# Attends and pieces put between the score groups, a new table of pieces, a ring of 28 row tiles

## The reference: what is computed

```python
def _L0_tok_ref(waveform, W, b, ln_gamma, ln_beta):      # 1500 rows of 256 an item
    x = waveform.reshape(B, T // RF, RF)
    h = jnp.einsum('bfr,hr->bfh', x, W) + b
    ...                                                  # layer norm with gamma, beta
    return h * 0.5 * (1.0 + jax.lax.erf(h / jnp.sqrt(jnp.float32(2.0))))
def _L0_attn_ref(x, Wq, bq, Wk, bk, Wv, bv, Wo, bo):     # 16 heads of 16
    Q, K, V = (proj(Wq, bq), proj(Wk, bk), proj(Wv, bv))
    scores = jnp.einsum('bhqd,bhkd->bhqk', Q, K) * scale
    attn = jax.nn.softmax(scores, axis=-1)
    out = jnp.einsum('bhqk,bhkd->bhqd', attn, V)
    ...
    return out @ Wo.T + bo
h = _L0_tok_ref(...)
h = h + _L0_attn_ref(_layernorm(h, axis=-1), ...)
h = h + _L0_ffn_ref(_layernorm(h, axis=-1), ...)         # ends in (y - mu) * rsqrt(var + 1e-05) * ln_g + ln_b
```

## Time and profile before

| what | us |
|---|---|
| time before, median of 3 runs | 2660.03 (2657.61 to 2660.93) |
| the profiled execution, its own time | 2662.67 |
| its span in the profile | 2660.6 |
| PE matmuls busy | 2317.9 (87%) |
| ACT busy | 2124.1 (80%) |
| DVE busy | 1083.9 (41%) |
| POOL busy | 363.6 (14%) |
| mean granted clock of PE | 0.947 of full |

### The profile page before, as it was taken

How to read it: one execution, slowest core, us unless ns; L and a number is a source line. 1 busy time by engine, 2 the same in 40 slices (tenths; PEclk the granted TensorE clock), 3 DMA queues, 4 the chain that set the end, 5 groups by cost and what they waited for, 6 DMA issues and landing times.

```text
span 2660.6 us, 39157 instructions
## 1 busy us (share of the span) xinstructions
PE 2317.9 (87%) x15468; PEld 738.9 (28%) x15468; DVE 1083.9 (41%) x1873; ACT 2124.1 (80%) x1562; POOL 363.6 (14%) x495
## 2 busy tenths in 40 slices
PE   4588998899978998889988899889998899988883
PEld 2222332222222222322223233222222222322221
DVE  6333434534344434443435343453434443442114
ACT  0198887888968888788877888788887888889992
POOL 2201101211021111201112011111102111110002
PEclk7799998999989999899999999899999899999997
DMA  2312211222121222122211221112212022121100
GB/s 63 100 32 70 68 42 40 58 64 65 41 66 31 67 71 57 49 57 63 60 40 49 72 72 43 41 49 72 65 43 63 26 65 74 51 56 43 36 12 29
DMA packets 102228, 144.12 MB, mean 54 GB/s; under 512 B 18439, under 2 KB 81990, under 8 KB 102014
## 3 DMA queue, kind: packets, MB, share of 16 engines
q1 hardware_dynamic: 99478, 139.42, 20.7%
q10 hardware_dynamic: 2536, 1.83, 0.3%
HBM read 55.16 MB, written 61.44 MB: 44 GB/s over the span
## 4 chain that ended last, share of the span: by engine, by line
issue 47%; PE 28%; POOL 10%; ACT 6%; DVE 3%; POOLq 1%; DMA 1%; SPq 1%; DVEq 1%; ACTq 0%
PE PS L744 12%; PE PS L720 8%; PE PS L683 6%; ACT prob L417 5%; POOL sq L329 3%; POOL Y L337 3%; POOL rs L339 2%; POOL rs L310 1%; DMA qk_halves_scratch<-HL 1%; DVE HL L483 1%; PE PS L691 1%; POOLq L338 1%; DVEq L527 1%; DVE HL L485 1%; SPq L209 1%
## 5 line engine op out<-in xcount | busy, mean ns | idle before, releaser
L417 ACT ACTIVATE prob<-PS 125x2000 f32<-125x2000 f32 x768 | 1411.1, 1837 | 136.7 <-PE PS L720 136.6
L744 PE MATMUL PS<-prob,Vst 125*32 125x500 f32 x9216 | 1154.1, 603 | 1.0
L422 ACT ACTIVATE prob<-PS 125x1000 f32<-125x1000 f32 x768 | 772.1, 1005 | 311.1 <-PE PS L720 296.9
L720 PE MATMUL PS<-QA,KA 64*125 64x500 f16 x4608 | 758.6, 409 | 194.6 <-ACT prob L417 140.4
L720 PEld LDWEIGHTS PS<-QA,KA 64*125 64x125 f16 x4608 | 257.0, 134 | 832.0 <-issue 419.9
L744 PEld LDWEIGHTS PS<-prob,Vst 125*32 125x32 f32 x9216 | 220.9, 109 | 536.0 <-issue 356.5
L526 DVE RECIPROCAL On<-Den 128x500 f32<-128x500 f32 x96 | 314.1, 3272 | 67.4 <-DMA Den<-Osb 67.4
L483 DVE TENSOR_SCALAR HL<-PS,b_qk 128x500 f16<-128x500 f32 x96 | 70.9, 739 | 425.8 <-PE PS L683 322.9
L329 POOL TENSOR_TENSOR sq<-HL 128x2000 bf16<-128x2000 f16 x24 | 84.5, 3521 | 981.3 <-DVE HL L485 981.3
L683 PE MATMUL PS<-zT,w_qk 128*128 128x500 f32 x384 | 210.6, 640 | 1.2 <-DVE zT L474 1.2
L710 PE MATMUL PS<-w_o,oT 128*125 128x256 f32 x384 | 122.0, 448 | 57.4 <-DVE Hs L444 35.2
(11 more groups left out here) (72 smaller groups left out, 899.6 us busy)
## 6 DMA issues: line engine op xcount, KB each, us to landing
qk_halves_scratch<-HL SPq DMA_DIRECT2D x384, 125.0 KB
QA<-qk_halves_scratch SPq DMA_DIRECT2D x64, 375.0 KB, 5.2
KA<-qk_halves_scratch SPq DMA_DIRECT2D x64, 375.0 KB, 7.2
Den<-Osb SPq DMA_DIRECT2D x384, 31.2 KB, 1.9
oT<-On SPq DMA_DIRECT2D x384, 31.2 KB, 1.9
out<-Y SPq DMA_DIRECT2D x24, 500.0 KB
X<-in_x SPq DMA_DIRECT2D x8, 468.8 KB, 4.0
w_qk<-in_wqT ACTq DMA_DIRECT2D x2, 128.0 KB, 3.7
```

Source lines behind the costliest of these rows:

```text
L417: act.activation(prob[0:T, 6 * p:6 * p + 4, :], PS[0:T, 0:4, 0:QC], ACT.Exp, scale=scl)\
L422: act.activation(prob[0:T, 6 * p + 4:6 * p + 6, :], PS[0:T, 4:6, 0:QC], ACT.Exp, scale=scl)\
L720: last = pe.matmul(PS[0:T, bank, 0:QC], KA[rows, G % 2, h // 2, t * T:(t + 1) * T], QA[rows, G % 2, h // 2, c * QC:(c + 1) * QC], start=Tr ...
L744: last = pe.matmul(PS[lo:lo + 2 * HD, 6 + n % 2, 0:QC], Vst[:, b % 2, t, g * HG + j, :], prob[0:T, (HG * t + j) % 12, :], start=(t == 0), ...
```

## The change

It has five parts.

1. In `unit` on PE the attends are placed anew. Even rounds: two score blocks, the third attend of the pair before (in round 0 the last attend of the unit before), the wait for A, four blocks, one attend, pieces. Odd rounds: two blocks, pieces, the wait for A, four blocks, one attend.
2. `PLAN` becomes a table of lists, with other places for nearly all pieces: most stand at rounds 1, 3, 4, 5 and 7, and three `out` pieces at (1, 7). `tok` of the item after the next begins at (10, 5).
3. `GELU` moves from (3, 2) to (1, 7), and the three normalisations from (3, 4), (5, 4), (7, 6) to (2, 1), (4, 4), (7, 4).
4. On DVE `invert` is called after round 1 in place of round 2, `finish_out` comes behind the next piece's take, and `take_sums` is for the unit whose last attend now stands in round 0.
5. `Hs` has 28 tiles used as a ring; GELU is split in two instructions where the rows wrap round its end. SP's stores of output and its load of `X` stand earlier in the unit.

```diff
-    PLAN = {}
+    PLAN = {(u, r): [] for u in range(NU) for r in range(PER)}
...
+    HRING = 2 * NT + CT
...
-    for j in range(4):
-        place(5, 3 + j, "val", j)
-    place(6, 0, "turn", 2)
-    place(6, 1, "norm", 0)
-    place(6, 2, "turn", 3)
...
+    place(2, 3, "turn", 0)
+    place(2, 4, "turn", 1)
+    place_qk(0, 2, 5, 7)
...
+    place(5, 1, "turn", 2)
+    place(5, 2, "norm", 0)
+    place(5, 3, "turn", 3)
...
+    NORMS = {(2, 1): 0, (4, 4): 1, (7, 4): 2}
+    GELU = (1, 7)
...
-                    if r == 2 and n > 0:
+                    if r == 1 and n > 0:
                         invert(n - 1)
...
+            def beside(b, u, r, bank, used):
+                for what, pb, i, last in pieces(b, u, r):
+                    if used == UNIT_USES[b * NU + u] and b + u > 0:
+                        pe.wait_ge(s_ov, b * NU + u)
+                    pe.wait_ge(s_free, used)
...
                 for r in range(PER):
-                    R = R0 + r
+                    R, q = R0 + r, r // 2
                     if R > 0:
                         pe.wait_ge(s_ex, 2 * R)
                     scores(n, 6 * r + 4, 2, exact_max)
+
+                    if r % 2 == 0 and q > 0:
+                        attend(n, 3 * q - 1)
+                    if r == 0 and u > 0:
+                        attend(n - 1, NT - 1)
+                    if r % 2 == 1:
+                        used = beside(b, u, r, bank, used)
                     pe.wait_ge(s_ex, 2 * R + 1)
                     if r < PER - 1:
                         scores(n, 6 * r + 6, 4, exact_max)
...
+                    attend(n, 3 * q + r % 2)
                     if r % 2 == 0:
-                        attend(n, 3 * q)
-                    else:
-                        attend(n, 3 * q + 1)
-                        pe.wait_ge(s_ex, 2 * R + 2)
-                        attend(n, 3 * q + 2)
-                    started = beside(b, u, r, started)
+                        used = beside(b, u, r, bank, used)
```

More of the change, by code:

```diff
@@ L42, in place_qk @@
         place(u, r1, "qk", i, True)
-    for j, r in enumerate((0, 2, 4, 6)):
+    for j, r in enumerate((1, 3, 4, 5)):
+        place(11, r, "out", j)
         place(0, r, "out", 4 + j)
[L46 to L56, removed]
@@ L76, in audio_tower @@
[L76 to L79, removed]
+    place(11, 7, "tok", 2)
+    place(0, 7, "tok", 3)
+    place(1, 1, "tok", 4)
+    place(1, 3, "tok", 5)
+    place(1, 5, "out", 8)
+    for j in range(3):
+        place(1, 7, "out", 9 + j)
+    place(2, 3, "turn", 0)
+    place(2, 4, "turn", 1)
+    place_qk(0, 2, 5, 7)
+    place_qk(1, 3, 1, 3)
+    place_qk(2, 3, 4, 5)
+    place(3, 7, "val", 0)
+    place_qk(3, 4, 1, 3)
+    place(4, 4, "val", 1)
@@ new lines, in audio_tower @@
+    place(4, 5, "val", 2)
+    place(4, 7, "val", 3)
+    place(5, 1, "turn", 2)
+    place(5, 2, "norm", 0)
+    place(5, 3, "turn", 3)
+    place_qk(4, 5, 4, 5)
+    place(5, 7, "val", 4)
+    place_qk(5, 6, 1, 3)
+    place_qk(6, 6, 4, 5)
+    place(6, 7, "val", 5)
+    place_qk(7, 7, 1, 3)
+    place(7, 4, "val", 6)
+    place(7, 5, "val", 7)
+    place(7, 7, "turn", 4)
+    place(8, 1, "turn", 5)
+    place(8, 2, "norm", 1)
+    place_qk(8, 8, 3, 4)
+    place_qk(9, 8, 5, 7)
+    place_qk(10, 9, 1, 3)
@@ L92, in audio_tower, with pieces @@
+    def pieces(b, u, r):
+        found = []
+        if b == 0 and u == 0 and r in (1, 3, 5):
+            found.append(("tok", 1, (r - 1) // 2, True))
+        for what, i, last in PLAN[u, r]:
+            pb = batch_of(what, b, u)
+            if 0 <= pb < B and (what == "out" or pb > 0):
+                found.append((what, pb, i, last))
+        return found
     USE = {}
@@ L107, in audio_tower @@
     FIRST = len(USE)
-    FILLED = {}
+    UNIT_USES = []
     for b in range(B):
         for u in range(NU):
+            UNIT_USES.append(len(USE))
             for r in range(PER):
[L112 to L115, removed]
+                for what, pb, i, last in pieces(b, u, r):
+                    if last:
+                        USE[what, pb, i] = len(USE)
     for i in range(4, NT):
@@ L262, in _ @@
                     load_group(b * NG + u // NC + 1)
+                if u < 3 and b > 0:
+                    store_out(b - 1, u)
+                if u == 2 and b + 2 < B:
+                    load_x(b + 2)
                 for r in range(PER):
[L264 to L268, removed]
+                    for what, pb, i, last in pieces(b, u, r):
+                        if what == "qk" and last:
+                            store_halves(pb, i)
                     if r == 2 and n > 0:
@@ L358, in _ @@
                     for r in range(PER):
[L359 to L368, removed]
+                        for what, pb, i, last in pieces(b, u, r):
+                            if what == "tok":
+                                root1(pb, i)
+                            if what == "out":
+                                out_root(pb, i)
+                            if what == "qk" and last and i % 4 == 3:
+                                squares(pb, i // 4)
+                        if b + 1 < B and (u, r) in NORMS:
+                            root2(b + 1, NORMS[u, r])
+                            add_bias(b + 1, NORMS[u, r])
             for e in range(4, NT):
@@ L591, in unit @@
                 bank = 7 - n % 2
+                if exact_max:
+                    row_max(n)
                 if n > 0:
                     take_sums(n - 1)
-                if exact_max:
-                    row_max(n)
                 finish = None
                 for r in range(PER):
[L598 to L617, removed]
-                    if r == 2 and n > 0:
-                        invert(n - 1)
-                    if b + 1 < B and (u, r) in ((3, 4), (5, 4), (7, 6)):
-                        norm_stats(b + 1, (u - 3) // 2)
-                        norm_apply(b + 1, (u - 3) // 2)
@@ new lines, in unit @@
+                    for what, pb, i, last in pieces(b, u, r):
+                        if what == "tok":
+                            tok_stats(pb, i, bank)
+                            tok_norm(pb, i, bank)
+                        if what == "turn":
+                            take_turn(pb, i, bank)
+                        if what == "qk" and last:
+                            take_qk(pb, i, bank)
+                        if what == "val":
+                            take_val(pb, i, bank)
+                        if what == "norm":
+                            take_norm(pb, i, bank)
+                        if what == "flag":
+                            take_flag(pb, bank)
+                        if what == "out":
+                            take_out(pb, i, bank)
+                        if finish is not None:
+                            finish_out(*finish)
+                        finish = (pb, i) if what == "out" else None
```

110 lines of the change are left out of this document (48 added, 62 removed).

## The result

The change is slower: 2725.59 us (median of 4 runs, 2718.64 to 2726.22) against 2660.48 us for the kernel before on the same chip. The ratio is 1.024, with a 95% interval of 1.022 to 1.0259. The forecast was 2705. The profiled execution has a span of 2724.2 us, 63.6 more than before; its mean granted clock is 0.947, as before.

A forecast was written before the change was run, and what follows sets the result against it. PE and ACT hold each other up, neither bound by busy time alone; each change of kind costs about 0.15 us. Six items add 32.4, the first 13.4, the last -0.8: about +45 on 2660, 2705 us, range 2645 to 2760.

The forecast's parts named there:

- The pairs: Two rounds on PE in the new order: 5.83 us with one heavy piece, 6.86 with two, 5.48 without.
- part 4: Invert after round 1 on DVE: waits an item of 5.0 us behind norms, 1.4 at unit 8's qk, 2.8 small ones.
- The rival of cheaper pairs: Two blocks beside a piece cost 0.15 us less on some 38 pairs in 7 items: 2665 us; chance 0.13.
- a change of kind would be free: Rival, all pairs on PE: switching instruction kind costs nothing, not about 0.15 us; run about 200 shorter, 2460; chance 0.02.
- The gain without a piece: Pairs of rounds without a piece take 5.48 us in place of 5.63, a gain of 0.15.
- The wait for z: Normalisation at (2, 1): PE stands 6.7 us at the turn, then a lower clock; together 8.6 us an item.
- T: Start of round 0 of unit 2 on PE, from which the times of the normalisation at (2, 1) were counted.
- The waits behind the norms: At (5, 2), (8, 2) and (10, 2), PE waits 1.8, 1.8 and 1.45 us behind DVE's reciprocal: 5.0 an item.
- The rival that short waits bring the lower clock too: Five waits an item of 1.4 us and more, each 2 us dearer by the clock: 70 more, 2775 us; chance 0.12.
- Before, two pieces in a pair: Kernel before, heavy pieces in both rounds: 6.43 us from its steps, so the new order at 6.86 loses 0.43.
- The passage between items: From A of (11, 7) to A of (0, 2), kept at 18.57 us for three rounds: adds 9.8 an item.
- The last item: No pieces in units 2 to 10, outs at (1, 7) without GELU over them: -0.8 us against before.

The follow-up runs named there:

- e6: Changed kernel with the third attend ahead of the two score blocks in even rounds, not behind them: 2654.64 us, ratio 0.9985 to the kernel before.
- e8: Changed kernel with invert after round 2 and the first normalisation at (2, 2), still behind the reciprocal: 2669.17 us, ratio 1.0034 to the kernel before.
- e2: Changed kernel with invert after round 2 in place of round 1, so also behind unit 2's normalisation: 2605.40 us, ratio 0.9793 to the kernel before.
- e1: Changed kernel with the first normalisation at (2, 0), ahead of the reciprocal, in place of (2, 1): 2654.35 us, ratio 0.9979 to the kernel before.
- e4: Changed kernel with PE's order of before and everything else of the change: 2885.16 us, ratio 1.0848 to the kernel before.

## Why the forecast was right in kind, and where it was short

- **The pairs.** Foreseen 5.83, measured 5.80 to 5.83; with two pieces 6.86 against 6.84 (unit 6, which takes 24.27 in place of 24.35). Two pieces of `val` or `out` at rounds 4 and 5 make 7.11: the 0.27 is one of the small waits of part 4. The cost of the two blocks ahead of a piece was taken as 0.36 and is 0.35. e6 shows it by its opposite. The rival of cheaper pairs falls. By the rule of the Trainium skill, page "TensorE: Matmul & The Clock Gate", section "Step-by-step: what each phase is for", that the emptying of the array after one matmul overlaps the filling by the next, a change of kind would be free. The trace disagrees: two blocks in front of a piece take 0.35, not 0.21.
- **The gain without a piece** was foreseen as 0.15 a pair; the last item's units 3 to 10 take 21.76 each against 22.52, so 0.19.
- **The wait for z** had every link right except its start. T is 831.34 in item 2; PE asked at T + 8.7 (847.79 less 7.71), as foreseen, but the sums were copied at T + 3.1 (834.42) and not T + 2.1, since DVE was still finishing the third `out` of (1, 7). So PE stood 7.7 and not 6.7. Price: 8.6 foreseen, 9.1 by e8 less e2, 10.2 by e1.
- **The waits behind the norms** are the term that was mis-sized. I gave the step 5.0 an item at the full clock; what e8 takes away is 8.1, and waits of 0.42 stay beside. The length of each wait in units 5 and 8 is the time from the copy to the reciprocal less 2.74: 1.81 where that time is the 4.54 of the earlier trace rows, as foreseen (the prediction's own times differ by 1.7, not the 1.8 that it states). Two things failed in it. The denominators' DMA took up to 6.0 us in place of 4.54, which made waits of up to 3.3; together the waits are 6.2 an item (43.1 us in 21 times). And the clock fell behind 11 of the 21: of the 8.1, 4.9 are waiting, so some 3 an item are work at the lower clock (by subtraction). The rival that short waits bring the lower clock too was half right: it held behind 9 of the 14 waits in units 5 and 8, and in items 0 to 6 of the profile after nowhere behind waits of 1.36 to 1.47.
- **Before, two pieces in a pair** I put at 6.43 from its steps; in units 4 and 7 one such pair takes 6.41 to 6.44 and the other 6.67 to 6.71. So the new order, at 6.84, loses less there than I said, 0.3 on the mean and not 0.43. Why the second is longer is not shown. This did not enter the sum, which went by the item of before as measured.
- **The sum.** Forecast for a middle item 322.9, measured 325.5; the first 318.8 and 321.5. The missing 19 us of the whole (63.6 of span against 45) are 7 x 2.6. Added up by units, the forecast is 3.5 too low in units 5, 8 and 10 (the norms) and 1.0 too low in unit 2 (z). The small waits, put at 2.8, come to about 2.9 in the other units.
- **The passage between items** was to stay, and is 2.0 too high in the forecast: from A of (11, 7) to A of (0, 2) are 16.6 us (mean of seven) and not 18.57, since PE stands 3.2 there and not 5.0. Why is not shown. That the sum is short by 2.6 an item and not by 4.6 is luck.
- **The last item** came out at -0.7 against -0.8, which is in part luck too: the pairs of units 3 to 10 gave 6.1 and not 4.8, and unit 1 with its three outs took 4.4 more than before.

## What to carry to other kernels

When two orders are compared on an engine that is always busy, count the groups of the same kind of instruction and price each change from a row: here eight groups in place of four ate what the order had won. When a table of pieces is moved, walk the engine that takes the pieces (here DVE) through the new places in its own order and note when each result is ready: a slow instruction with a DMA ahead of it, put before a short one that another engine waits for, costs more than its own length. Order and table are one thing: each alone was 5% to 8% slower (e4, the table alone, still holds the waits for z and behind the norms), and the mends that paid, 3.4% better than before, were one table entry, one round's number and two statements exchanged.

## What was not expected of the hardware

The granted clock fell after shorter waits of PE than the rows of before had shown. After 2.94 us in one case it had stayed high. In the profile after, at the same place (5, 3) of items 0 and 6, with the same rows ahead of them, it once stayed and once fell behind a wait of 1.81 us:

```profile
270.30 0.65 PE L696 MATMUL PS<-ident,z 125*128 125x125 f32 x4 [1.81 <-DVE nmx L513]
270.87 0.64 PE L739 MATMUL PS<-QA,KA 64*125 64x500 f16 x4
...
2228.29 0.85 PE L696 MATMUL PS<-ident,z 125*128 125x125 f32 x4 [1.81 <-DVE nmx L513]
2229.07 1.09 PE L739 MATMUL PS<-QA,KA 64*125 64x500 f16 x4
```

Behind the first turn PE goes on at 2.4 GHz (0.64 for four blocks), behind the second at 1.2 (1.09). What decides between them is open; in e1 one wait of 3.11 us was followed by the full clock. Behind waits of 1.36 to 1.47 us no row of items 0 to 6 of this profile shows a fall; but in e2 and e8 the clock fell at (1, 7) of item 1, behind waits of 0.52, 1.46 and 0.65 us close together. The DMA of the denominators, the same four transfers each time, took from 4.5 to 6.8 us from the copy's start to the reciprocal's, where the reciprocal waited for it; which traffic beside it makes the difference was not tried.
